# Cross-attention over 16 sequences: where GpSimd cuts its x pieces and the output weights, and where five query products stand in the first slots

## The reference

```python
q = heads(x @ to_q_w)
# the context tokens fall in four groups: 77 text, 4 object, 4 others, the remaining 427 "ip",
# each with key and value weights of its own
h_g = softmax(q @ heads(ctx_g @ to_k_g_w).T / sqrt(32)) @ heads(ctx_g @ to_v_g_w)
out = (h_txt + h_obj + h_oth + h_ip) @ to_out_w + to_out_b + x
```

## Time and profile before

| | |
|---|---|
| median of 3 runs (lowest, highest) | 2437.27 us (2437.21, 2443.76) |
| the profiled execution, its own time | 2437.21 us |
| its span in the trace | 2435.6 us |
| TensorE's mean granted clock, share of full | 0.994 |
| busy: TensorE, VectorE, ScalarE, GpSimd | 98%, 76%, 73%, 17% of the span |

### The profile page before, as it was taken

How to read it: one execution, slowest core, us unless ns; L and a number is a source line. 1 busy time by engine, 2 the same in 40 slices (tenths; PEclk the granted TensorE clock), 3 DMA queues, 4 the chain that set the end, 5 groups by cost and what they waited for, 6 DMA issues and landing times.

```text
span 2435.6 us, 37404 instructions
## 1 busy us (share of the span) xinstructions
PE 2389.4 (98%) x12801; PEld 1806.8 (74%) x12801; DVE 1845.9 (76%) x3288; ACT 1778.7 (73%) x3909; POOL 412.3 (17%) x567
## 2 busy tenths in 40 slices
PE   7999999999999998999999999999999999999998
PEld 7899999998999984566666666666666666666654
DVE  3356777732333478999999999999999999999992
ACT  3243433322222359999999999999999999999994
POOL 0000000000000023423133133122133132222210
PEclk9999999999999999999999999999999999999999
DMA  9545444374644657677677677677687677677751
GB/s 283 145 144 165 152 141 141 124 255 144 231 160 175 202 134 148 133 142 146 132 150 156 128 147 153 136 151 148 132 156 147 130 151 155 132 148 140 146 127 50
DMA packets 346820, 370.10 MB, mean 152 GB/s; under 512 B 94334, under 2 KB 241918, under 8 KB 346630
## 3 DMA queue, kind: packets, MB, share of 16 engines
q1 hardware_dynamic: 293232, 304.79, 56.0%
q10 hardware_dynamic: 53398, 62.93, 7.5%
HBM read 215.57 MB, written 83.89 MB: 123 GB/s over the span
## 4 chain that ended last, share of the span: by engine, by line
PE 87%; DVE 6%; ACT 4%; issue 1%; ACTq 1%; DMA 1%; SPq 0%
PE st_ps L1499 16%; PE s_ps L440 11%; PE om_ps L492 11%; PE st_ps L460 11%; PE om_ps L474 11%; PE om_ps L515 8%; PE s_ps L1551 7%; PE om_ps L1551 4%; PE s_ps L1519 3%; PE st_ps L1551 3%; DVE negmax L668 2%; ACT s_ps L608 2%; ACT probs L600 1%; ACTq L1222 1%; DMA qpack<-q_out 1%
## 5 line engine op out<-in xcount | busy, mean ns | idle before, releaser
L608 ACT ACTIVATE s_ps<-s_ps,negmax 128x427 f32<-128x427 f32 x1280 | 768.8, 609 | 23.3 <-DVE small L677 23.2
L668 DVE TENSOR_REDUCE negmax<-s_ps 128x2 f32<-128x854 f32 x640 | 666.2, 1041 | 81.8 <-PE s_ps L440 74.0
L600 ACT ACTIVATE probs<-st_ps 128x1024 f32<-128x1024 f32 x632 | 656.8, 1039 | 28.0 <-PE st_ps L460 13.0
L1499 PE MATMUL st_ps<-ctx_split,w_split 128*128 128x428 f32 (+2 forms) x2280 | 432.5, 350 | 11.2 <-DVE k_out L1379 10.8
L1499 PEld LDWEIGHTS st_ps<-ctx_split,w_split 128*128 128x128 f32 x2280 | 413.2, 191 | 29.2 <-DVE k_out L1379 11.9
L440 PE MATMUL s_ps<-kpack,qpack 96*128 96x512 f32 x1280 | 423.6, 412 | 10.8 <-ACT s_ps L608 7.5
L460 PE MATMUL st_ps<-qpack,kpack 104*128 104x512 f32 x1264 | 408.6, 404 | 8.7 <-ACT probs L600 8.5
L400 POOL TENSOR_TENSOR small<-small,negmax 128x616 f32<-128x616 f32 x160 | 196.4, 1227 | 1084.1 <-DVE negmax L685 1084.0
L440 PEld LDWEIGHTS s_ps<-kpack,qpack 96*128 96x128 f32 x1280 | 221.8, 189 | 194.3 <-ACT s_ps L608 91.1
L492 PE MATMUL om_ps<-xs,wq 128*128 128x512 f32 x1200 | 342.2, 395 | 5.0 <-DVE out L748 4.1
L515 PE MATMUL om_ps<-heads,wo 128*128 128x512 f32 x1125 | 322.8, 394 | 0.0
(11 more groups left out here) (103 smaller groups left out, 2318.4 us busy)
## 6 DMA issues: line engine op xcount, KB each, us to landing
kpack<-kT SPq DMA_DIRECT2D x240, 256.0 KB, 4.2
qpack<-q_out SPq DMA_DIRECT2D x240, 256.0 KB, 7.6
kT<-k_out ACTq DMA_DIRECT2D x160, 217.5 KB, 3.3
ctx_split_raw<-in_ctxT SPq DMA_DIRECT2D x128, 214.0 KB, 4.6
tok_pair<-in_ctxT SPq DMA_DIRECT2D x48, 512.0 KB, 4.4
xs_raw<-in_xT SPq DMA_DIRECT2D x85, 256.0 KB, 5.3
out<-in_xT SPq DMA_DIRECT2D x75, 256.0 KB, 5.6
out_yT<-out SPq DMA_DIRECT2D x75, 256.0 KB, 2.2
```

The lines of the kernel that those rows point to most:

```text
L600: nc.scalar.activation(probs[:, at:at + 2, :], transposed(u, duo), ACT.Exp).then_inc(p_done, 1)
L608: last = nc.scalar.activation(s_ps[:, n % 2, z, SMALL:TOK], s_ps[:, n % 2, z, SMALL:TOK], ACT.Exp, bias=negmax[:, r, IP, j, t:t + 1], accu ...
L668: nc.vector.tensor_reduce(negmax[:, r, IP, j, t0:t0 + 2], s_ps[:, n % 2, :, SMALL:TOK], AX_X, ALU.max, negate=True).then_inc(s_max, 1)
L1499: last = nc.tensor.matmul(k_place(run, m)[:, 0:n], w[name][:, pw, q, m * P:(m + 1) * P], c[b][:, px, q, a:a + n], start=(q == 0 and z == 0 ...
```

## The change

Two things are moved; no instruction is added or taken away.

GpSimd: in the slots in which a sequence's x is cut, `less_max(w + 2, 0)` stands behind two chunks instead of three, so that chunks 2, 3 and 4 come behind it. Of the output weights, three chunks are cut in slot 3 ahead of `less_max(5, 1)`, where there were two ahead of it and one behind it.

TensorE: in slots 0, 2, 3 and 4, step 5 has two query products instead of three, step 6 two instead of four, and step 7 three instead of none.

```diff
-Q_AHEAD_FIRST = {2: (0, 3), 3: (3, 7), 5: (8, 11), 6: (11, 15)}
+Q_AHEAD_FIRST = {2: (0, 3), 3: (3, 7), 5: (8, 10), 6: (10, 12), 7: (12, 15)}
...
             if x_due:
-                for c in range(3):
+                for c in range(2):
                     split_x(m, c)
             if unit(w + 2):
                 less_max(w + 2, 0)
             if x_due:
-                for c in range(3, QC):
+                for c in range(2, QC):
                     split_x(m, c)
-            for c in {3: (0, 1), 4: (3, 4)}.get(w, ()):
-                split_wo(c)
+            if w in (3, 4):
+                for c in ((0, 1, 2), (3, 4))[w - 3]:
+                    split_wo(c)
             if unit(w + 2):
                 less_max(w + 2, 1)
-            if w == 3:
-                split_wo(2)
```

## The result

| | before | changed |
|---|---|---|
| median, beside each other on one chip | 2439.62 us (4 runs) | 2463.43 us (4 runs, 2462.13 to 2473.61) |
| ratio | | 1.0102, 95% interval 1.0087 to 1.0118 |
| the profiled execution, its own time | 2437.21 us | 2463.14 us |
| its span, mean granted clock | 2435.6 us, 0.994 | 2461.5 us, 0.988 |

The change makes the kernel 1.0% slower. In the profiled executions it costs 25.9 us where 16.6 were forecast; the time lies above the forecast range of 2446 to 2458.

A forecast was written before the change was run, and what follows sets the result against it. TensorE was taken to bound the kernel, with VectorE's add_output on the path in x slots. 15.1 (x slots) + 1.5 (slot 3) + 0 (TensorE's products) = 16.6 us, giving 2453.8 us, +0.7%; 8-in-10 range 2446 to 2458.

The forecast's parts named there:

- Where the limit lies: Ordinary slots: TensorE is busy for all 18.63 us, its waits aren't won back; in x slots a late add_output lengthens them.
- VectorE beside GpSimd: VectorE's small instructions L698, L701, L703 stretch to the end of a GpSimd instruction beside them: about 0.68, 0.53, 1.37 us.
- the rival in which it gets ahead: x slots: L703 starts before GpSimd's subtraction and stays short; +1.0 us, slot 3 +0.3, total 2438.5, no change; chance 8%.
- The term of the x slots: add_output starts 1.40 us later; thirteen x slots last 20.42 us each, slot 71 stays at 20.96; +15.1 us.
- the clock falls: x slots: granted clock halves after each TensorE rest for as long as the rest; 21 us more, 2475; chance 2%.
- Slot 3: Moved output-weight chunk catches L701 and L703, ScalarE's exponentials start late and hold up TensorE; +1.5 us, bounds 0 and 1.8.
- TensorE's products: Slots 0, 2, 3, 4: three products moved behind the last scores fill TensorE's idle time; 0, at most 2.7 us either way.
- slot 1: Cuts x too, but no add_output exists yet and L703 already took 1.37 us; no effect.
- the need of x: Query products: chunk 4's halves are ready at 1043.2 instead of 1041.3, but only step 7 multiplies them; no effect.
- The faster rival: GpSimd's last pair falls wholly behind VectorE's small instructions, thirteen x slots return to 18.63 us; -8.1 us, 2429.1; chance 2%.

The follow-up runs named there:

- the run with the reduction: Kernel before, with one VectorE reduction of 1280 columns put ahead of the addition in x slots, GpSimd's order untouched: ratio 1.0111, 2461.87 us.
- the first profile: First profiled execution of the changed kernel, with the whole change against the kernel before: 2463.14 us against 2437.21.
- the last experiment: Kernel before, with GpSimd in x slots waiting for VectorE's third small instruction before cutting the last chunk: ratio 0.9978, 2433.42 us against 2438.65.
- first filled run: Changed kernel, with the two score products of step 4 made four times in x slots: ratio 1.0083 against the kernel before.
- the second run: Changed kernel measured once more, unaltered, beside the same kernel with repeated score products: ratio 1.0112 against the kernel before, 2466.79 us.
- the addition first: VectorE makes add_output ahead of neg_lse in step 4, against the kernel before: ratio 1.0041; with the old rows of x also asked for earlier, 1.0062.

## Why the prediction was wrong

- *Where the limit lies*: right. Ordinary slots stay at 18.63, and what makes the addition late lengthens x slots one for one, in the change and in the run with the reduction.
- *VectorE beside GpSimd*: right. In slot 51 a chunk landed 0.48 us late for GpSimd, the first small instruction took 1.20 us instead of 0.68, and the slot 0.5 us more: I had expected such a landing to cost nothing. L703's race is lost in all fourteen slots of the first profile; the rival in which it gets ahead fell.
- *The term of the x slots*, +15.1: mis-sized, and this is the step that failed. Forecast were 13 x 20.42 + 20.96 = 286.4 us, measured 293.76. The five with a fallen clock take 110.33 us instead of 102.10, +8.2; slot 71 takes 20.38 instead of 20.96, -0.6, since the addition now comes later than the packed queries; the other eight are 0.3 under the forecast. The miss in this term is the clock's.
- *The rival "the clock falls"* had 2%. Its price for one rest, 1.5 us, came out, but in part by luck: it was to follow the rest's length, and slot 16, which rested 1.73 us, is busy for the same 20.42 us as slot 26, which rested 1.49. It struck five or six of fourteen. The argument against it was one rest of 1.44 us with a clock of 1.00. One example can't exclude what strikes one rest in three: nine of fourteen rests of the changed kernel also leave the clock alone. The range, too, should have held the case of "some of them fall": 2453.8 + 5 x 1.5 is 2461.3.
- *Slot 3*: right by +1.5 in two runs; 0.8 more in the first profile, where TensorE rested 1.55 us and the clock fell.
- *TensorE's products, slot 1, the need of x*: nothing that the runs can tell, as forecast.
- *The faster rival*: its mechanism was real, but this change doesn't bring it; it needs the last chunk behind L703, which the last experiment does by a wait.
- *The ends*: the +3 us of slots 76 and 77 and the -1.6 ahead of slot 0 can't be put down to the change. Slot 0 began between 921.23 and 928.58 us over all kernels. Slot 76 lasted from 18.61 us (with the reduction) to 22.42 (first filled run) over all kernels, at clocks from 1.00 to 0.77, 22.39 in the run that beats both.

Not settled: why a rest of 1.5 us is followed by a fallen clock in these slots and not in others. The length doesn't decide it: in the run with the reduction, slots 11, 51 and 56 rested 2.0 to 2.3 us at a clock of 1.00. In the changed kernel's x slots each fall begins 0.5 to 1.0 us after the product that ends the rest.

## What to carry to other kernels

A stream with spare time isn't free: look at what its instructions do to those of a neighbour that the critical engine waits for, and hold them back with a wait rather than by order. If a change makes a busy TensorE rest 1.5 us where it didn't, price the rest and, in a part of the cases, about as much again for the clock. One undisturbed example is no proof that there is no fall; a range must hold some of them falling.

## What the runs showed of the hardware

- *Rests and the clock.* After a rest of 1.5 us the granted clock fell to 1.2 GHz in 5 or 6 of 14 places for 3 to 4 us, and cost 1.5 us (20.42 against 18.91 busy; in slot 71 of the second run twice as much, 21.91); with TensorE kept busy, in none of 28. Two profiled executions of the changed kernel had the same five places, and the runs with only the x slots' order and with the reduction partly others; whether a third execution would repeat them isn't shown. The Trainium skill's page "TensorE: Matmul & The Clock Gate", section "A second HAM failure mode: psum-queue depth-cycling", tells of a clock that goes back and forth when TensorE rests briefly and often between groups of matmuls. This trace agrees on the brief rests, but here they needn't be frequent: they are single and 95 us apart.
- *Transfers in a queue.* Asking for one block of rows ahead of the new sequence's x took the 8.3 us of waits for them from VectorE and raised GpSimd's waits for x from 12.3 to 34.9 us, both with the addition first.
